# Attention kernel with quantised layers: the codes of three weights made earlier and passed through DRAM, and one sum moved from GpSimd to TensorE

## The reference

```
x   : 8 batches of 512 tokens by 512;  ctx: the same shape
x = x + tanh(g_xattn[0]) * (MHA(layernorm(x), ctx, ctx) @ W_O + b_O)   # 16 heads of 32
x = x + tanh(g_ffn[0]) * down(silu(gate(layernorm(x))) * up(layernorm(x)))   # inner 2048
x = x + tanh(g_xattn[1]) * softmax(layernorm(x) @ ctx.T) @ ctx
x = x + tanh(g_ffn[1]) * (fp4(x) @ fp4(weight).T + bias)

gate, up, down: weight codes clip(round(w * scale), -1, 1), scale = 1 / mean(|w|) over the whole matrix
fp4: per block of 32, scale = 2^(floor(log2(max)) - 2) * 2^d, values rounded to steps of FP4
```

## Time and profile before

| | |
|---|---|
| median of 3 runs | 1636.88 us (1634.34 to 1637.41) |
| profiled execution, its own time | 1635.9 us |
| its span, first to last instruction | 1634.1 us |
| PE busy | 1475.7 us (90%), 6969 matmuls |
| DVE busy | 1241.7 us (76%) |
| ACT busy | 874.5 us (54%) |
| POOL busy | 918.9 us (56%) |
| DMA queue | 257.85 MB, 55.4% of 16 engines |
| attention phase | to about 888 us |

### The profile page before, as it was taken

The page is one execution under the profiler, slowest core; times in us unless marked ns, Lnnn a source line. Parts: engine busy times, 40 slices in busy tenths (PEclk is TensorE's granted clock), DMA queues, the critical chain, the costliest instruction groups (busy, mean ns, idle before and its releaser), DMA issues. The chain is left out here.

```text
span 1634.1 us, 24705 instructions
## 1 busy us (share of the span) xinstructions
PE 1475.7 (90%) x6969; PEld 932.6 (57%) x6969; DVE 1241.7 (76%) x2141; ACT 874.5 (54%) x1434; POOL 918.9 (56%) x1160
## 2 busy tenths in 40 slices
PE   5699999899998999999674899999999978999997
PEld 4466556566565656566321455555555546877785
DVE  3567787877879767767664688888888858998996
ACT  4265556565555565555543455555555545655552
POOL 3166676585675676665555343433344326778775
PEclk9899999999999999999765999999999999999998
DMA  5836749375583846648765244444444564556531
GB/s 174 252 111 195 225 149 269 99 230 170 162 245 121 260 138 194 186 123 242 197 181 154 72 114 109 106 108 109 115 108 110 150 189 132 165 159 202 168 87 62
DMA packets 247020, 259.03 MB, mean 159 GB/s; under 512 B 140028, under 2 KB 156936, under 8 KB 243208
## 3 DMA queue, kind: packets, MB, share of 16 engines
q1 hardware_dynamic: 246920, 257.85, 55.4%
HBM read 149.50 MB, written 76.58 MB: 138 GB/s over the span
## 5 line engine op out<-in xcount | busy, mean ns | idle before, releaser
L704 ACT ACTIVATE a_probs<-a_sc 128x512 f32<-128x512 f32 x512 | 300.2, 595 | 295.4 <-PE a_sc L600 294.2
L789 DVE TENSOR_REDUCE a_negmax<-a_mx 128x1 f32<-128x512 f32 x512 | 337.6, 674 | 94.6 <-PE a_mx L583 93.6
L914 POOL TENSOR_TENSOR a_acc<-a_acc,a_probs 128x512 f32<-128x512 f32 x256 | 330.7, 1323 | 21.5 <-ACT a_probs L704 20.8
L914 POOL TENSOR_TENSOR a_acc<-a_probs 128x512 f32<-128x512 f32 x128 | 166.3, 1318 | 256.8 <-ACT a_probs L704 255.9
L583 PE MATMUL a_mx<-a_stack 96*128 96x512 f32 x512 | 230.6, 450 | 52.3 <-DVE a_negmax L789 40.4
L600 PE MATMUL a_sc<-a_stack 97*128 97x512 f32 x512 | 218.6, 429 | 24.9 <-ACT a_probs L704 18.0
L1065 PE MATMUL bank<-wcode,b_xq 128*128 128x512 bf16 x1024 | 228.1, 381 | 7.8 <-DMA b_xq<-b_xcode 7.8
L1065 PEld LDWEIGHTS bank<-wcode,b_xq 128*128 128x128 bf16 x1024 | 100.3, 98 | 130.9 <-DMA b_xq<-b_xcode 9.7
L583 PEld LDWEIGHTS a_mx<-a_stack 96*128 96x128 f32 x512 | 101.1, 198 | 128.6 <-DVE a_negmax L789 78.9
L795 DVE RECIPROCAL a_attn<-a_den 128x128 f32<-128x128 f32 x128 | 120.9, 948 | 59.8 <-PE a_den L628 59.8
L1103 ACT ACTIVATE b_sig<-bank,b_tok 128x512 f32<-128x512 f32 x128 | 87.6, 684 | 90.6 <-PE bank L1065 88.5
(11 more groups left out here) (165 smaller groups left out, 2646.7 us busy)
## 6 DMA issues: line engine op xcount, KB each, us to landing
a_stack<-spill SPq DMA_DIRECT2D x192, 256.0 KB, 4.8
spill<-k_part SPq DMA_DIRECT2D x64, 512.0 KB, 3.5
ctx_t<-k_wo SPq DMA_DIRECT2D x16, 1024.0 KB, 8.1
c_ct<-ctx_t SPq DMA_DIRECT2D x8, 2048.0 KB, 8.5
a_stage<-in_x_dram SPq DMA_DIRECT2D x32, 256.0 KB, 5.0
a_stage<-in_ctx_dram SPq DMA_DIRECT2D x32, 256.0 KB, 2.7
attn_t<-a_attn SPq DMA_DIRECT2D x32, 256.0 KB, 4.4
b_xin<-in_x_dram SPq DMA_DIRECT2D x32, 256.0 KB, 2.7
```

What stands on the lines that cost most here:

```text
L704: nc.scalar.activation(probs[:, k, j, :], sc[i % 2][:], ACT.Exp, scale=SCALE).then_inc(exp_done, 1)
L789: nc.vector.tensor_reduce(negmax[:, g % 2, j, t:t + 1], mx[i % 2][:], axis=AX.X, op=ALU.max, negate=True).then_inc(mx_done, 1)
L914: nc.gpsimd.tensor_tensor(acc[:, j], probs[:, 0, j] if k == 1 else acc[:, j], probs[:, k, j], ALU.add)\
```

## The change

What it does:
- Of the last batch's work only the transposes stay, twelve of them, now read from a new DRAM tensor `code_t`. The codes are made one piece ("unit") in a group, in groups 14, 15, 16, 18, 19, 20, 22, 23, 24, 26, 27 and 28 (group n is group n mod 4 of batch n div 4): a load of 1 MB, two halves on ACT behind the last score's exponential, three DVE operations, and a store of half a megabyte. The load of a unit waits until the codes of the one before are stored, since all share `wsum`.
- The absolute sums are taken in groups 1 to 12, 2,048 columns each, and the three scales follow in batch 3.
- The last layer's weight is quantised in batch 0, in 30 DVE operations: six on all 2,048 columns before the first maxima, 24 on 512 columns, spread behind the first 20 maxima.
- W_O is split by one operation each on ACT and DVE, in the last batch.
- In the last group of the last batch POOL adds nothing; PE sums the exponentials with 16 `ones` matmuls straight out of `probs`, and the `pv` matmuls are spread between the scores.
- `JOIN` is 3165 in place of 3190.

```
-    CH, SUMS, RAWS = 4, 8, 3
+    UNITS = 3 * CH
+    SUM_FIRST, QSTEPS = 1, 6 + 6 * C
+    CODE_IN = {n: k for k, n in enumerate((14, 15, 16, 18, 19, 20, 22, 23, 24, 26, 27, 28))}
...
-            ck.add(base + 20, 9, "sload", g)
-            ck.add(base + BURST + 2, 9, "sum", g)
-        ck.add(BURST + at["den"], 9, "wscale")
-        ck.add(-60, 9, "wload1")
-        for n in range(QSTEPS):
-            ck.add(PERIOD * (n // 6) + BURST + n % 6, 9, "wquant", n)
-        ck.add(2 * PERIOD + 30, 9, "wstore1")
-        for k, tick in enumerate(ITEM_AT):
-            ck.add(tick, 9, "rload", k)
-            for h in range(2):
-                ck.add(tick + 30 + 6 * h, 9, "rround", k, h)
-            ck.add(tick + 40, 9, "rclip", k)
-            ck.add(tick + 44, 9, "rcode", k)
-            ck.add(tick + 50, 9, "rturn", k)
+            ck.add(base + BURST + 26, 9, "uload", g + 1, "sum")
+            if g != 1:
+                ck.add(base + (-36 if g == 2 else 38), 9, "uload", g, "code")
+            ck.add(base + BURST + 2, 9, "sum", g, 0)
+            ck.add(base + BURST + 10, 9, "sum", g, 1)
+            ck.add(base + BURST + 2, 9, "uround", g, 0)
+            ck.add(base + BURST + 10, 9, "uround", g, 1)
+            ck.add(base + BURST + 12, 9, "uclip", g, 0)
+            ck.add(base + BURST + 20, 9, "uclip", g, 1)
+            ck.add(base + BURST + 29, 9, "ucode", g)
+            ck.add(base + BURST + 44, 9, "ustore", g)
+            if g < T - 1:
+                for n, tick in enumerate((5, 35, 65, 100)):
+                    ck.add(base + tick, 9, "uturn", g, n)
+        for k, tick in enumerate((74, 88, 112, BURST + 14)):
+            ck.add((G - 1) * PERIOD + tick, 6, "pv_last", G - 1, k)
...
+                        if n in CODE_IN and args[1] == "code":
+                            k = CODE_IN[n]
+                            if k:
+                                sp.wait_ge(u_stored, 16 * k)
...
+                        sp.wait_ge(u_code, k + 1)
+                        sp.dma_start(code_t[k].rearrange("p (a n) -> p a n", a=4), codes).then_inc(u_stored, 16)
...
+                        sp.dma_start_transpose(wcode[:, k], code_t[k]).then_inc(gu_turned if k < 2 * CH else down_turned, 16)
...
+                def add_up(k):
+                    for j in range(J):
+                        last = nc.tensor.matmul(den[DH * j:DH * (j + 1), :], ones[:], probs[:, k, j, :], start=k == 0, stop=k == T - 1)
+                    return last
...
+                    elif name in ("pv", "pv_last"):
...
+                        if final and k < T - 1:
...
+                            add_up(k)
...
+                def quantise(n):
+
+                    c, step = (n - 6) // 6, n if n < 6 else 6 + (n - 6) % 6
+                    u, m = wsum[:], wmag
+                    if n >= 6:
+                        u, m = u[:, c * D:(c + 1) * D], m[:, c * D:(c + 1) * D]
+                    if n:
+                        dve.wait_ge(q_step, n)
...
+                        slot_n = g * T * J + i - 1
+                        if it + shift == 0 and 0 <= slot_n < 5 * C:
+                            if slot_n % 5 == 0:
+                                quantise(6 + slot_n // 5 * 6)
+                            quantise(6 + slot_n // 5 * 6 + 1 + slot_n % 5)
...
-                    elif name == "acc":
+                    elif name == "acc" and not (it + shift == NB - 1 and args[0] == G - 1):
...
-    JOIN, SCALE = 3190, 0.64
+    JOIN, SCALE = 3165, 0.64
```

More of the change, by code:

```diff
@@ L263, in attention_phase @@
         nmean = sb("nmean", [P, T], F32)
-        sums = sb("sums", [P, 3 * SUMS], F32)
+        sums = sb("sums", [P, 2 * UNITS], F32)
         wtot = sb("wtot", [P, 3], F32)
@@ L267, in attention_phase, with unit @@
         scale_w = sb("scale_w", [P, 3], F32)
-        cw = sb("cw", [P, C, NBL], F32)
-        e2 = sb("e2", [P, NBL], F32)
-        ie = sb("ie", [P, NBL], F32)
+        e2, ie, cw = (attn[:, 0, n * C * NBL:(n + 1) * C * NBL] for n in range(3))
         brow = mrow[0:3 * G, 0, :].bitcast(F32)
         wsrc = [m.rearrange("(o p) i -> p o i", p=P) for m in ffn_w]
-        raws = [nc.alloc_sbuf_tensor_at(f"raw{n}", [P, 2048], F32, offset=place["xt"] + 8192 * n)[:] for n in range(2)] + [wsum[:]]
-        codes = nc.alloc_sbuf_tensor_at("codes", [P, 2, 2048], BF16, offset=place["stage"])[:]
-        wraw, wmag = wsum[:, 1024:1024 + D], wsum[:, 1024 + D:1024 + 2 * D]
+        codes = nc.alloc_sbuf_tensor_at("codes", [P, 4, 1024], BF16, offset=place["wsum"])[:, :, 0:512]
+        wmag = probs[:, T - 1].rearrange("p j s -> p (j s)")
+        def unit(k):
+            per = wsrc[k // CH].shape[1] // CH
+            return per, wsrc[k // CH][:, k % CH * per:(k % CH + 1) * per, :]
         work = [pb("work0"), pb("work1")]
@@ new lines, in window @@
+                    elif name == "sum" and SUM_FIRST <= (it + shift) * G + args[0] < SUM_FIRST + UNITS:
+                        g, h = args
+                        k = (it + shift) * G + g - SUM_FIRST
+                        half = wsum[:, h * 1024:(h + 1) * 1024]
+                        if h == 0:
+                            act.wait_ge(s_loaded, 16 * (k + 1))
+                        nc.scalar.activation(half, half, ACT.Abs, accum_out=sums[:, 2 * k + h:2 * k + h + 1]).then_inc(summed, 1)
+                    elif name == "uround" and (it + shift) * G + args[0] in CODE_IN:
+                        g, h = args
+                        k = CODE_IN[(it + shift) * G + g]
+                        half = wsum[:, h * 1024:(h + 1) * 1024]
+                        if h == 0:
+                            act.wait_ge(u_loaded, 16 * (k + 1))
+                            if k == 0:
+                                act.wait_ge(w_scaled, 1)
+                        nc.scalar.activation(half, half, ACT.Copy, scale=scale_w[:, k // CH:k // CH + 1], bias=ROUND).then_inc(u_round, 1)
+                    elif name == "wohigh" and it + shift == NB - 1:
+                        act.wait_ge(wo_loaded, 16)
+                        act.wait_ge(v_full, T * NB)
+                        act.wait_ge(ct_stored, NB * 32)
+                        nc.scalar.activation(wo[:, :, HI, :], wsum[:].rearrange("p (c e) -> p c e", c=C), ACT.Copy).then_inc(wo_hi, 1)
@@ L782, in window @@
                                                        part[:, side, HI, :].bitcast(F32), ALU.add, ALU.subtract).then_inc(qk_lo, 1)
+                        if it + shift == 0 and (g, side) == (1, Q):
+                            dve.wait_ge(exp2_done, 2)
+                            dve.wait_ge(gated, 1)
+                            for n in range(3, 6):
+                                quantise(n)
                     elif name == "max":
```

267 lines of the change are left out of this document (117 added, 150 removed).

## The result

The changed kernel took 1623.75 us (median of 5 runs, 1620.84 to 1625.93), the kernel before 1636.09 (median of 5, two more than were known for the prediction). The ratio is 0.9929 with a 95% interval of 0.9918 to 0.9939: faster by 0.7%, about 12 us. I had forecast 1612 and a range of 1598 to 1626. The time lies inside the range, but the gain is only half of the forecast one, 12 us in place of 25. So the account has to be opened step by step.

What follows compares the result with a forecast made beforehand. The last batch's weight work was taken to starve PE through DVE, ACT and POOL. A to F summed to -25.1 us from 1635.9, giving 1610.8; with the median 1.0 above, the forecast was 1612 us, range 1598 to 1626.

Steps and rivals of the forecast that it cites:

- B: Group 3 of batches 3 to 6: the 1 MB load ahead of the fills costs +10.2 us, between 0 and 14.8.
- F: Seam before the down matmuls: scores and third-phase turns fill PE's wait for `b_hq`, -2 us, between -4 and +1.
- A: Last batch, weight work gone except transposes: three groups at 23.2 us, the last 19.1 plus 4.9; -33.5 us.
- C: Batches 1 to 4: the quantiser leaves them, -10 us, between -11.6 and -5.
- D: The eight units outside group 3: DVE operations and ACT halves cost 0.9 us each, +7.2, bounds 0 and 20.
- E: Prologue: thirty quantise operations on DVE before and between the first maxima, +3 us, between 0 and +9.
- SP standing at the store: SP's in-order queue: a load waiting for a store holds the next batch's spills and fills; likeliest error, no size given.
- the rival of dear units: Eight units outside group 3 cost 20 us in place of 7.2, total 1625 us; chance 0.15.
- as the rival had it: Last batch: DRAM transposes, in smaller pieces, bind above 7.7 us each; 1622 us at twice 4.3; chance 0.07.
- that B and D don't appear: Group 3's load and the other eight units cost nothing, total 1595 us; chance 0.12.
- that the change does nothing: Last batch stays at 32 us a group, held by clock and ring; total 1638 us; chance 0.04.

Runs made afterwards that it cites:

- experiment 3: Changed kernel with the third and fourth transposes of the last batch's first group put behind the next `mrow` in SP's queue: 1619.23 us.
- experiment 9: Changed kernel with the last group's sum back on POOL and its `pv` steps behind the scores: 1626.87 us.
- experiment 4: Changed kernel with the four units of group 3 left out whole, the transposes reading others' codes: 1605.01 us.
- Experiments 6 and 7: Changed kernel with group 3's load at tick 22 instead of 38, 1607.28 us; and with group 3's units made in group 1, 1605.84 us.
- experiment 10: Kernel with units in group 1, late transposes and `JOIN` 3190 (1596.5 us), with the units' clips and code step 12, 12 and 9 ticks later: 1606.17 us.
- experiment 5: Changed kernel without the units' DVE work, ACT writing zeros that SP stores: 1624.01 us.
- Experiment 2: Kernel before with only `JOIN` changed, 3165 in place of 3190: 1638.28 us, ratio 1.0015.

## Why the prediction was right about the bound and wrong about the gain

The forecast missed the trace's difference by 12.9 us (-25.1 and -12.2). B makes 8.3 of them, F 5.9 and A 2.6; C with D and E came out 2.4 and 1.5 better than forecast. The step that failed is the price of a load as its bytes over the mean rate of the queue: "1.05 MB at 285 GB/s are 3.7 us. I take 3.0, as holes in the stretch absorb some". The runs showed 18.5 us for four units in place of 10.2, because everything behind the load in the queue landed later. The second is F, forecast as a gain of 2 because the new order fills one wait; it cost 1 to 4.

**The reading of what bound the kernel was right.** The weight work in the last batch starved PE. Without it groups take 21.1 and 22.1 us there instead of 32.0 and 30.6, and POOL's additions take 1286 ns instead of 1549.

**A (-33.5; -30.9 measured)** was right in sum only because two errors stood against each other. The step that failed in A is "I price the first three groups as the first group of batch 5". The first took 31.9, not 23.2: transposes out of DRAM held SP's queue for 7.28 and 5.41 us ahead of `mrow`, shown by experiment 3. It explains 6.3 of these 8.7 us (31.9 to 25.6). Against that the second and third took 43.2, not 46.4, and the last with its tail 21.1, not 24.0, its exponentials at a clock of 1.00 where I had reckoned with the lower level. That clock is luck: the other traces with the PE sum took 22.5 to 23.9 there. What the PE sum is worth stays open (experiment 9: 3.1 us, not clear of the spread).

**B (+10.2; 18.5 measured)** is the term that failed most. Comparing the changed kernel (407.1 us in batches 3 to 6) with experiment 4 (388.6) gives 18.5 us for four units, of which the four windows of group 3 hold 15.6 (112.7 against 97.1). The place was right: spill, fills, `mrow`, and no slack. The size was wrong because I divided the load's bytes by the mean rate and took "3.0, as holes in the stretch absorb some". There were no holes behind the load (DMA shares of 1.02 and 1.07 from 548 to 560 us); the hole lay in front of it (0.48). The spill lost 5.4 us, and the earlier fills, on which the maxima wait, about 4. The queue explains why all of them lost: of the 458 DMAs of the attention phase whose landing is in the trace, only one landed before the DMA issued just ahead of it, so what was issued behind the megabyte landed behind it too. Experiments 6 and 7 show it from the other side: same bytes, other place, 16.5 and 17.9 us less. SP standing at the store, which I had named as the likeliest error, was not it here; the store had landed before. In experiment 10 it had a part.

**C and D (-10 and +7.2).** In batches 1 and 2 the quantiser's leaving gave 195.3 - 191.1 = 4.2 us, so -10 for four batches was a little high. With experiment 4, eight units cost what C had put on batches 3 and 4, about 5 us, or 0.6 each. The bounds were needlessly wide, and the rival of dear units falls: it had put D at 20 us, and experiment 5, which took all the units' DVE work away, gained nothing. POOL was slow in the last batch before, as that rival said, but the clips of the unit there took 686 ns now, not 2316. The lock between DVE and GpSimd of which the Trainium skill speaks (SBUF — State Buffer, section "SBUF: two separate sides") showed behind group 0 of batch 5: a clip that began beside one of POOL's additions took 1.11 us, the next, beside none, 0.69. The trace agrees with that rule there, and it is worth 0.4 us. Over the changed kernel's trace five of the 24 clips began with 0.25 to 0.79 us of an addition left, and they took 0.80 to 1.34 us, longer the more was left; the other nineteen took 0.66 to 0.70.

**E (+3; +1.5)** was within its bounds. PE waited 3.29 us for the first `mrow` after other work had filled in.

**F (-2; between +1 and +4)** had the wrong sign. Experiment 2 is the clean one: +2.5 us on the kernel before by the ratio, 1.6 by the medians. The part behind attention took 750.2 to 755.9 us in nine traces with 3165 and 748.7 to 750.5 in five with 3190. I had seen one wait and a filler for it. PE's rows at the changed seam show where the filler's neighbours went:

```profile
1301.29 8.63 PE L1089 MATMUL bank<-wcode,b_xq 128*128 128x512 bf16 x32 [4.57 <-DMA b_xq<-b_xcode]
...
1312.57 3.01 PE L1503 MATMUL bank<-c_ct,c_xt 128*128 128x512 f32 x12 [2.20 <-DVE b_hid L1181]
...
1324.46 4.61 PE L1503 MATMUL bank<-c_ct,c_xt 128*128 128x512 f32 x12 [4.12 <-DVE c_xt L1601]
```

The wait of 5.76 us for `b_hq` is gone, as forecast, and waits of 4.57, 2.20 and 4.12 us stand there now, for the quantised input and for DVE; the kernel before had 1.55 and 2.39 us there, for `c_xt`, beside the 5.76. The order at the seam makes them: the fourteen traces fall into two sets by `JOIN` alone. With 3190 PE waits 3.8 to 5.8 us for `b_hq`, and its waits over 0.8 us, from 15 us before the third phase's first matmul to 60 us behind it, add up to 11.1 to 13.1 us. With 3165, on the kernel before too, it waits 1.9 to 5.4 us for `b_xq`, 2.2 for `b_hid` and 2.4 to 2.5 for `c_w`, none of which is over 0.8 in that stretch with 3190, and the sum is 14.9 to 18.5 us. Whether F costs as much in the changed kernel as in the one before stays open: the pairs with 3190 and 3165 there differ by less than their intervals.

**The rivals.** The transposes took longer in the changed kernel, a median of 6.1 us against 4.3. By the Trainium skill (DMA: Bandwidth & Descriptors, section "Where 436 GB/s comes from") I had estimated 5.2. No run separates the source from the fuller queue, but the last one, issued at 836.89 after 10 us without another transpose, reads

```profile
wcode<-code_t SPq DMA_TRANSPOSE x1, 4.5
```

so by this row most of the difference is the fuller queue and not the DRAM, and the estimate was too high for a transpose that stands alone. Nor were the pieces smaller, as the rival had it: the view of 768 to 842 us has 25,337 packets under 512 B with twelve transposes, that of 768 to 880 us before 23,264 with eleven. The median is below the 7.7 us at which they would have bound the end, and the last was issued 22 us before the last score. But they cost time in a way that the rival did not name, by holding SP. The rivals that B and D don't appear, and that the change does nothing, both fell.

## What to carry to other kernels

A transfer is not priced by its bytes but by what stands behind it in its queue: look at the DMA share just before and just after its place, and follow the next transfer on which an engine waits. Here 16 ticks on one load were worth more than the whole change had brought. A store that the next load waits for ties a vector operation to the spills of the following batch, so moving that operation can delay the store by 1.6 us and lengthen the group by 3 to 4.5 (experiment 10). And a wait that a reordering fills is only half of its price: name the next three waits as well, before calling it a gain.

## What the hardware showed that I had not expected

A DMA transpose held the queue of the engine that issued it: 2.1 to 7.3 us for each of the twelve out of DRAM, longest where the DMA share was at 1.05, against 0.4 to 0.8 us for a plain spill or store of as many bytes. In the kernel before, out of SBUF, the same instruction held it 1.5 to 5.7 us, mostly 1.8 to 2.0. A spill of half a megabyte landed after 2.8 to 13.1 us in the one trace of the changed kernel; the five longest are those behind a megabyte's load in a group 3. DMAs of this queue landed in the order of their issue, with one exception in 458. And the variation between executions of one kernel, 1.9 to 14.5 us from lowest to highest, was mostly larger than the 0.2% that I had named as what a measurement can tell.
